# Cross-attention, first batch: other places for the first halves of ctx and of a weight, an earlier weight load, and fill transposes between the row dots

## The chip, the cores and the metric

The kernel runs on one core of one Trainium2 chip. The metric is the device time of one execution in microseconds, the median of several runs. Lower is better.

## The reference, cut to what matters

For x and ctx of shape (8, 512, 512) the first layer is a cross-attention with gate, all in fp32, and a second layer (an attention with experts) follows. Only the first batch of the first layer is touched.

```python
e = layernorm(x)                                             # the "encoder" rows, per batch
Sim = (e @ w1)[:, :, None] + (ctx @ w2)[:, None, :] + einsum('bid,bjd->bij', e * w3, ctx) + b_sim[0]
A = softmax(Sim, axis=2)
hq = einsum('bij,bjd->bid', A, ctx)
hc = einsum('bi,bid->bd', softmax(max(Sim, axis=2), axis=1), e)[:, None, :]
x1 = x + tanh(g_xattn[0]) * (concat([e, hq, e * hq, e * hc]) @ W_qv + b_qv)
out = x1 + tanh(g_ffn[0]) * ffn(layernorm(x1))               # second layer, not touched
```

## The kernel before, in words

Every product of 512 x 512 x 512 is made in three passes (PASSES): each fp32 operand is split into a high half, a rounded copy written by ScalarE (ACT), and a low half, the difference, written by VectorE (DVE) or GpSimd (POOL). So every operand costs one "hi" and one "lo" operation per tile, [128 x 512] each, before TensorE (PE) may read it. A product of one row tile is 12 matmuls of 128x512.

The order of each engine is written out by hand, and each engine runs it strictly in that order; semaphores tie them together. SP issues the DMAs in the order of its own program.

The first batch has its own order:

- SP loads x(0), ctx_t(0), small rows, ctx(0), the weight block wh_raw (it lives in `spare[:, 0]`), then the four tiles of x(1), each behind a wait for et_ps. Then it waits for ct_lo, for ew1_biased (the row dots with their bias, a DVE operation in `first_dots` of the vector engine), loads the residual (1 MB into x_sb), waits for c_lo = NT and loads weh_raw (1 MB) into `spare[:, 1]`, where ctx(0) lay before.
- PE turns the normalised rows (turn_e), makes the scores of four row tiles, turns the probabilities (turn_a), makes the row dots e @ w1 as matmuls with one column (`first_dots(t)`: four 128x1 matmuls for a tile; L932), and then `first_feats`: four products attend(k) into ps_h (k = 0 to 3, between them the small row_weights steps), then the products feats(t, part) with the weights wh, weh and wec. attend(k) for k >= 2 waits for eh_ready = k - 1, because ps_h has two banks.
- ACT writes the hi halves: ctx tiles 0 and 1 early, 2 and 3 late; then, behind the last probs_hi, the four tiles of wh, the four of e_t2 (rows_hi), the gate and the bias row, the four of weh; then `attended`: for each k a copy of ps_h (h_t2 hi), and the hi half of eh.
- DVE, in `attended`, writes the low half of h_t2 and the product eh, which is what releases ps_h (eh_ready).
- POOL writes the low halves of ctx, then, behind a wait for newton (the reciprocal root for batch 1, done by DVE), of wh, weh, and in turn of eh and e_t2.
- `fill(n)` issues n transposes of the identity into ps_b whose result nobody reads.

The wait that the load of the second weight stands behind, in SP's program:

```python
load_x(1, second=True)
sp.wait_ge(ct_lo, ND)
sp.wait_ge(ew1_biased, 1)
load_residual(0)
sp.wait_ge(c_lo, NT)
sp.dma_start(weh_raw[:], w_blocks[2]).then_inc(weh_loaded, 16)
```

Of the kernel before, what the change touches and what calls it, by code (L numbers as in the profile page):

```python
# [28 lines left out]
P = 128  # L29
# [81 lines left out]
def cross_attention(nc, block, both, x, ctx, ctx_t, g_xattn, w_sim, w_sim_cols, b_sim, w_qv, b_qv, x1, w_vsd, wq, wk):  # L111
# [7 lines left out]
    with ExitStack() as mem:  # L119
# [162 lines left out]
        def _(sp):  # L282
# [55 lines left out]
            load_first_ctx_t()  # L338
            sp.dma_start(w1_row[:], w_sim[0:D].partition_broadcast(P)).then_inc(dots_loaded, 16)
            sp.dma_start(bsim_col[:], b_sim.partition_broadcast(P)).then_inc(dots_loaded, 16)  # L340
            load_first_ctx()
            sp.dma_start(gate_raw[:], g_xattn.partition_broadcast(P)).then_inc(bias_loaded, 16)
            sp.dma_start(bias_row[:], b_qv.partition_broadcast(P)).then_inc(bias_loaded, 16)
            sp.dma_start(wh_raw[:], w_blocks[1]).then_inc(wh_loaded, 16)
            load_x(1, second=True)
            sp.wait_ge(ct_lo, ND)
            sp.wait_ge(ew1_biased, 1)
            load_residual(0)
            sp.wait_ge(c_lo, NT)
            sp.dma_start(weh_raw[:], w_blocks[2]).then_inc(weh_loaded, 16)  # L350

# [19 lines left out]
        def _(pool):  # L371
# [7 lines left out]
            def ctx_lo(b, first=False):  # L379
                for t in range(NT):  # L380
                    pool.wait_ge(c_hi, b * NT + t + 1)
                    take_lo(pool, c_2, t, weh_raw if first else stage).then_inc(c_lo, 1)
# [10 lines left out]
            def rows_lo(b):  # L393
                for k in range(ND):
                    row_lo(b, k)

# [18 lines left out]
            ctx_lo(0, True)  # L415
            pool.wait_ge(newton, 2 * ROOT_STEPS)
            weight_lo(wh, wh_raw, 0, range(ND))
            weight_lo(weh, weh_raw, ND, range(ND))
            for k in range(ND):
                scaled_lo(0, k)  # L420
                row_lo(0, k)
# [31 lines left out]
        def _(act):  # L453
# [31 lines left out]

            def softmax_exp(b, t):
                act.wait_ge(nmax_ready, b * NT + t + 1)
                if t >= 2:

                    act.wait_ge(at_ps, b * NT + t - 1)  # L490
                act.activation(a_sb[:, t % 2, :], ps_s[:, t % 2, :], ACT.Exp, bias=nmax[:, t:t + 1],
                               accum_out=den[:, t:t + 1]).then_inc(a_exp, 1)
# [16 lines left out]
            def attended(b, first, more):  # L509
# [4 lines left out]
                for k in range(ND):  # L514
# [8 lines left out]
                    act.activation(eh_t2[:, 0, k, :], tmp[:, k, :], ACT.Copy).then_inc(eh_hi, 1)  # L523
                for k in range(ND):
# [17 lines left out]
            def first_softmax():  # L542
# [4 lines left out]
                ctx_hi(0, True, (0, 1))  # L547
                first_scaled_hi(1)
                copy_e(0, 1, True)
                softmax_exp(0, 0)  # L550
# [7 lines left out]
                copy_e(0, 3, True)  # L558
                probs_hi(0, 1)
                softmax_exp(0, 2)  # L560
                normalise(0, 2)
                ctx_hi(0, True, (2, 3))
# [4 lines left out]
                weights_hi(wh, wh_raw, wh_loaded, range(ND))  # L567
                rows_hi(0, range(ND))
                act.wait_ge(bias_loaded, 2 * 16)
                act.activation(gate[:], gate_raw[:], ACT.Tanh).then_inc(gate_ready, 1)  # L570
                act.wait_ge(gate_ready, 1)
                act.activation(bias_row[:], bias_row[:], ACT.Copy, scale=gate[:, 0:1]).then_inc(bias_ready, 1)
# [31 lines left out]
        def _(dve):  # L604
# [50 lines left out]
            def first_scaled_lo(t):  # L655
                cols = slice(t * P, (t + 1) * P)
                dve.wait_ge(es_ready, t + 1)
                dve.wait_ge(es_hi, t + 1)
                dve.tensor_tensor(es_t2[:, 1, :, cols], tmp[:, :, cols], es_t2[:, 0, :, cols].bitcast(F32),  # L659
                                  ALU.subtract).then_inc(es_lo, 1)  # L660

# [59 lines left out]
            def first_softmax():  # L721
# [38 lines left out]
                for part in range(5, ROOT_PARTS):  # L760
                    root(1, part)

# [134 lines left out]
        def _(pe):  # L897
# [14 lines left out]
            def fill(times):  # L912

                for _ in range(times):
                    pe.transpose(ps_b[:, 0:P], ident[:], ident[:])
# [128 lines left out]
            def softmax(b, first):  # L1044
# [6 lines left out]
                for t in range(NT):  # L1051
# [6 lines left out]
                    if first and t == NT - 1:  # L1058
                        first_dots(1)
                        first_dots(2)  # L1060
                    turn_a(b, t, first)
                if first:
                    first_dots(NT - 1)
# [902 lines left out]
```

## Time and profile before

| | us |
|---|---|
| median of 3 runs | 1227.55 (1226.86 to 1227.98) |
| the profiled execution's own time | 1226.06 |
| its span, first to last instruction | 1224.3 |
| PE busy | 1192.7 (97%) |
| DVE, ACT, POOL busy | 832.2, 642.4, 661.9 |

The span is what the trace covers; 1.8 us of the profiled execution's time lie around it. All times in the trace are microseconds from the span's start. Durations in the profile's rows are those of one execution, which was 1.5 us below the median of the runs.

### The profile page before, as it was taken

The numbers are of one execution on the slowest core, as the hardware profiler recorded it, in microseconds if no ns is written. First come the engines' busy times: TensorE is split into PE (matmuls) and PEld (weight loads), VectorE is DVE, ScalarE is ACT, GpSimd is POOL, SyncE is SP. The second block draws the span as 40 slices with busy tenths as digits, with TensorE's granted clock in tenths as the row PEclk, the third lists the DMA queues.
The fourth block names the chain that finished last, engine by engine and source line by source line (L and its number), as shares of the span: only waits on it lengthen the run. The fifth ranks groups of instructions, "written<-read, shape, count | busy, mean of one in ns | idle before, by whom it ended". The sixth has DMA issues, their size and how long they took to land.

```text
span 1224.3 us, 19821 instructions
## 1 busy us (share of the span) xinstructions
PE 1192.7 (97%) x6406; PEld 920.1 (75%) x6406; DVE 832.2 (68%) x1530; ACT 642.4 (52%) x1431; POOL 661.9 (54%) x481
## 2 busy tenths in 40 slices
PE   7899999999999999999999999999999999999995
PEld 6688888888888888876877768777777777777663
DVE  7587777777777765566576574766765765865766
ACT  5443434343434343466666566566656666665661
POOL 1744242424242425239469388297496495693893
PEclk9799999999999999999999999999999999999998
DMA  5431313141313132420102003002002010010010
GB/s 190 138 121 52 121 52 126 46 129 43 129 43 129 43 95 78 150 76 1 35 1 83 20 0 103 0 17 86 0 35 68 0 69 34 0 69 0 0 69 35
DMA packets 40749, 75.92 MB, mean 62 GB/s; under 512 B 3728, under 2 KB 4240, under 8 KB 40720
## 3 DMA queue, kind: packets, MB, share of 16 engines
q1 hardware_dynamic: 40720, 75.55, 18.6%
q8 instruction: 16, 0.26, 0.1%
q14 instruction: 13, 0.11, 0.0%
HBM read 58.76 MB, written 16.78 MB: 62 GB/s over the span
## 4 chain that ended last, share of the span: by engine, by line
PE 91%; DVE 4%; issue 1%; ACT 1%; DMA 1%; POOLq 0%; POOL 0%; SPq 0%; DVEq 0%
PE ps_f L908 19%; PE ps_r L1802 15%; PE ps_s L1859 9%; PE ps_o L1872 9%; PE ps_s L1851 8%; PE ps_s L908 7%; PE ps_h L908 7%; PE ps_r L1811 6%; PE ps_r L1835 5%; PE ps_r L1817 1%; PE ps_t L961 1%; PE ps_r L1793 1%; PE ps_r L1825 1%; DMA spare<-in_w_qv 1%; PE ps_t L926 1%
## 5 line engine op out<-in xcount | busy, mean ns | idle before, releaser
L1564 DVE TENSOR_REDUCE nmax<-ps_s 128x1 f32<-128x512 f32 x256 | 158.7, 682 | 112.2 <-PE ps_s L1851 111.9
L1438 ACT ACTIVATE tmp<-ps_s,nmax 128x512 f32<-128x512 f32 x256 | 172.7, 688 | 106.7 <-DVE nmax L1564 106.7
L1399 POOL TENSOR_TENSOR z<-z,z_tmp 128x1280 f32<-128x1280 f32 x40 | 117.2, 2929 | 173.6 <-DVE z_tmp L1578 170.9
L1381 POOL TENSOR_TENSOR spare<-xv,pick 128x512 f32<-128x512 f32 x160 | 168.2, 1051 | 33.0 <-DVE pick L1673 19.9
L1387 POOL TENSOR_TENSOR spare<-spare 128x512 f32<-128x512 f32 x128 | 180.4, 1410 | 10.0
L1447 ACT ACTIVATE pt<-ps_s 128x512 f32<-128x512 f32 x256 | 132.4, 619 | 10.7 <-PE ps_s L1859 10.7
L1859 PE MATMUL ps_s<-ident,tmp 128*128 128x128 f32 x1024 | 125.0, 273 | 2.6 <-ACT tmp L1438 2.5
L1859 PEld LDWEIGHTS ps_s<-ident,tmp 128*128 128x128 f32 x1024 | 115.1, 140 | 13.6 <-ACT tmp L1438 6.9
L255 POOL TENSOR_TENSOR e_t<-e_t 128x512 fp32r<-128x512 f32 x32 | 40.7, 1298 | 141.5 <-ACT e_t L484 141.5
L1872 PE MATMUL ps_o<-pt,spare 128*64 128x512 f32 x512 | 116.9, 598 | 0.0
L1851 PE MATMUL ps_s<-k,q 64*128 64x512 f32 x768 | 106.9, 409 | 2.2 <-DVE k L1620 1.5
L908 PE MATMUL ps_h<-es_t,c 128*128 128x512 f32 x384 | 101.2, 415 | 4.3 <-DVE tmp L815 4.2
L1851 PEld LDWEIGHTS ps_s<-k,q 64*128 64x128 f32 x768 | 67.2, 184 | 46.2 <-issue 34.0
L1802 PE MATMUL ps_r<-es_t,wk 128*128 128x512 f32 x384 | 97.1, 401 | 0.0
L1802 PE MATMUL ps_r<-es_t,c_t 128*128 128x512 f32 x384 | 96.6, 400 | 0.0
L255 POOL TENSOR_TENSOR c<-stage,c 128x512 fp32r<-128x512 f32 x28 | 42.4, 1548 | 100.2 <-ACT c L251 100.2
L908 PE MATMUL ps_s<-c_t,es_t 128*128 128x512 f32 x384 | 93.8, 396 | 1.3 <-DVE es_t L659 1.2
L908 PE MATMUL ps_f<-weh,eh_t 128*128 128x512 f32 x384 | 94.7, 396 | 0.0
L908 PE MATMUL ps_f<-wh,h_t 128*128 128x512 f32 x384 | 93.7, 393 | 0.4 <-DVE x_sb L850 0.4
L908 PE MATMUL ps_f<-wec,e_t 128*128 128x512 f32 x384 | 92.3, 393 | 0.4 <-DVE wec L255 0.4
L908 PEld LDWEIGHTS ps_h<-es_t,c 128*128 128x128 f32 x384 | 73.2, 198 | 20.7 <-DVE tmp L815 4.3
L1802 PEld LDWEIGHTS ps_r<-es_t,wk 128*128 128x128 f32 x384 | 70.3, 188 | 21.0 <-issue 5.8
(198 smaller groups left out, 2114.3 us busy)
## 6 DMA issues: line engine op xcount, KB each, us to landing
stage<-in_x SPq DMA_DIRECT2D x32, 256.0 KB, 3.1
x_sb<-in_x SPq DMA_DIRECT2D x8, 1024.0 KB, 5.3
x_dram<-x_sb SPq DMA_DIRECT2D x32, 256.0 KB, 2.4
stage<-x_dram SPq DMA_DIRECT2D x8, 1024.0 KB, 5.6
x_sb<-x_dram SPq DMA_DIRECT2D x8, 1024.0 KB, 5.5
out_dram<-x_sb SPq DMA_DIRECT2D x32, 256.0 KB, 2.0
stage<-in_ctx_t SPq DMA_DIRECT2D x28, 256.0 KB, 3.0
stage<-in_ctx SPq DMA_DIRECT2D x28, 256.0 KB, 2.7
```

The source lines that it names most:

```text
L255: return eng.tensor_tensor(pair[:, 1, k, :], operand[:, k, :], pair[:, 0, k, :].bitcast(F32), ALU.subtract)
L908: last = pe.matmul(out, left(l, k), right(r, k), start=start and n == 1, stop=stop and n == ND * len(PASSES))
L1381: pool.tensor_tensor(v_tmp[:] if e else acc, xv[:, :, e, :].unsqueeze(2).broadcast_to(shape), pick[:, 0, e, :, 2 * p:2 * p + 2].unsqueeze( ...
L1387: pool.tensor_tensor(acc, acc, v_tmp[:], ALU.add).then_inc(v_steps, 1)
L1399: pool.tensor_tensor(zv, zv, z_tmp[:, h % 2], ALU.add).then_inc(z_pool, 1)
L1438: act.activation(probs[:, n % BANKS, :], ps_s[:, n % BANKS, :], ACT.Exp, bias=nmax[:, n:n + 1], accum_out=den[:, h, t:t + 1]).then_inc(p_e ...
L1447: act.activation(pt[:, h % 4, :, t * P:(t + 1) * P], ps_s[:, n % BANKS, :].rearrange("p (k t) -> p k t", k=NT), ACT.Copy).then_inc(pt_read ...
L1564: dve.tensor_reduce(nmax[:, n:n + 1], ps_s[:, n % BANKS, :], AX_X, ALU.max, negate=True).then_inc(nmax_ready, 1)
L1802: end = pe.matmul(ps, w2[:, l, k, n * P:(n + 1) * P], y_t2[:, r, k, :], start=m == 0, stop=m == len(every) - 1)
L1851: end = pe.matmul(ps_s[:, (n + a) % BANKS, :], q2[head_rows(a), p % 2, l, t * P:(t + 1) * P], k2[head_rows(a), p % 2, r, :], start=m == 0, ...
L1859: end = pe.transpose(ps_s[:, n % BANKS, k * P:(k + 1) * P], probs[:, n % BANKS, k * P:(k + 1) * P], ident[:])
L1872: end = pe.matmul(ps_o[head_rows(a), :], v_acc[:, p, k, a, :], pt[:, p % 2 * 2 + a, k, :], start=k == 0, stop=k == NT - 1)
```

## The change

It concerns the first batch of the cross-attention alone.

- SP: ctx(0) and wh_raw are issued ahead of the small rows (b_sim, w1, the gate, the bias); these come behind x(1). The load of weh_raw waits for c_lo = NT only, and the residual comes behind it; the wait for ew1_biased is gone.
- ACT: all four hi halves of ctx at once; the four of wh one by one at three earlier places; e_t2's hi halves are cut by row tiles (`first_row_hi(t)`, 128 columns of all four k) instead of by k, two of them behind the last probs_hi, two inside `attended`; gate and bias behind the k loop.
- POOL: a wait for es_lo = NT before ctx tiles 2 and 3; three low halves of wh ahead of the wait for newton; two row tiles of e_t2 (`first_row_lo`) instead of four tiles.
- DVE: the low halves of the other two row tiles of e_t2, read from PSUM, behind the reciprocal root of batch 1.
- PE: fifteen more fill transposes around the last row dots and turn_a(3); all fills write another quarter of ps_b.

```diff
--- before.py
+++ after.py
@@ -336,18 +336,17 @@
             load_x(0, True)
             sp.dma_start(w_cols[:], w_sim_cols).then_inc(cols_loaded, 16)
             load_first_ctx_t()
+            load_first_ctx()
+            sp.dma_start(wh_raw[:], w_blocks[1]).then_inc(wh_loaded, 16)
+            load_x(1, second=True)
+            sp.dma_start(bsim_col[:], b_sim.partition_broadcast(P)).then_inc(dots_loaded, 16)
             sp.dma_start(w1_row[:], w_sim[0:D].partition_broadcast(P)).then_inc(dots_loaded, 16)
-            sp.dma_start(bsim_col[:], b_sim.partition_broadcast(P)).then_inc(dots_loaded, 16)
-            load_first_ctx()
             sp.dma_start(gate_raw[:], g_xattn.partition_broadcast(P)).then_inc(bias_loaded, 16)
             sp.dma_start(bias_row[:], b_qv.partition_broadcast(P)).then_inc(bias_loaded, 16)
-            sp.dma_start(wh_raw[:], w_blocks[1]).then_inc(wh_loaded, 16)
-            load_x(1, second=True)
-            sp.wait_ge(ct_lo, ND)
-            sp.wait_ge(ew1_biased, 1)
-            load_residual(0)
             sp.wait_ge(c_lo, NT)
             sp.dma_start(weh_raw[:], w_blocks[2]).then_inc(weh_loaded, 16)
+            sp.wait_ge(ct_lo, ND)
+            load_residual(0)
             sp.wait_ge(w_lo, ND)
             sp.dma_start(we_raw[:], w_blocks[0]).then_inc(wraw_loaded, 16)
@@ -376,8 +375,8 @@
             pool.affine_select(out=ident[:], in_=ident[:], compare_op=ALU.not_equal, fill=1.0, base=0,
                                pattern=[[-1, P]], channel_multiplier=1).then_inc(ident_ready, 1)
-            def ctx_lo(b, first=False):
-                for t in range(NT):
+            def ctx_lo(b, first=False, tiles=range(NT)):
+                for t in tiles:
                     pool.wait_ge(c_hi, b * NT + t + 1)
                     take_lo(pool, c_2, t, weh_raw if first else stage).then_inc(c_lo, 1)
@@ -393,6 +392,12 @@
             def rows_lo(b):
                 for k in range(ND):
                     row_lo(b, k)
+
+            def first_row_lo(t, copies):
+                cols = slice(t * P, (t + 1) * P)
+                pool.wait_ge(et_hi, copies)
+                pool.tensor_tensor(e_t2[:, 1, :, cols], e_t[:, :, cols], e_t2[:, 0, :, cols].bitcast(F32),
+                                   ALU.subtract).then_inc(et_lo, 1)
             def scaled_lo(b, k):
                 pool.wait_ge(eh_hi, b * ND + k + 1)
@@ -412,13 +417,19 @@
             pool.wait_ge(es_lo, NT - 1)
-            ctx_lo(0, True)
+            ctx_lo(0, True, (0, 1))
+            pool.wait_ge(es_lo, NT)
+            ctx_lo(0, True, (2, 3))
+            weight_lo(wh, wh_raw, 0, (0, 1, 2))
             pool.wait_ge(newton, 2 * ROOT_STEPS)
-            weight_lo(wh, wh_raw, 0, range(ND))
+            weight_lo(wh, wh_raw, 0, (3,))
             weight_lo(weh, weh_raw, ND, range(ND))
-            for k in range(ND):
-                scaled_lo(0, k)
-                row_lo(0, k)
+            scaled_lo(0, 0)
+            scaled_lo(0, 1)
+            scaled_lo(0, 2)
+            first_row_lo(0, 3)
+            scaled_lo(0, 3)
+            first_row_lo(3, 4)
             pool.wait_ge(wec_ready, ND)
             add_bias(0, 0)
@@ -483,6 +494,10 @@
                 for k in tiles:
                     act.activation(e_t2[:, 0, k, :], e_t[:, k, :], ACT.Copy).then_inc(et_hi, 1)
+            def first_row_hi(t):
+                cols = slice(t * P, (t + 1) * P)
+                act.activation(e_t2[:, 0, :, cols], e_t[:, :, cols], ACT.Copy).then_inc(et_hi, 1)
+
             def softmax_exp(b, t):
                 act.wait_ge(nmax_ready, b * NT + t + 1)
                 if t >= 2:
@@ -521,6 +536,13 @@
                                        accum_out=bsum[:, 0:1]).then_inc(bexp_ready, 1)
                     act.wait_ge(eh_ready, b * ND + k + 1)
                     act.activation(eh_t2[:, 0, k, :], tmp[:, k, :], ACT.Copy).then_inc(eh_hi, 1)
+                    if first and k < 2:
+                        first_row_hi(3 * k)
+                if first:
+                    act.wait_ge(bias_loaded, 2 * 16)
+                    act.activation(gate[:], gate_raw[:], ACT.Tanh).then_inc(gate_ready, 1)
+                    act.wait_ge(gate_ready, 1)
+                    act.activation(bias_row[:], bias_row[:], ACT.Copy, scale=gate[:, 0:1]).then_inc(bias_ready, 1)
                 for k in range(ND):
                     act.wait_ge(wec_ready, b * ND + k + 1)
                     act.activation(wec[:, 0, k, :], tmp[:, k, :], ACT.Copy).then_inc(wec_hi, 1)
@@ -544,9 +566,10 @@
                     ctx_t_hi(0, k, True)
                 first_scaled_hi(0)
                 copy_e(0, 0, True)
-                ctx_hi(0, True, (0, 1))
+                ctx_hi(0, True)
                 first_scaled_hi(1)
                 copy_e(0, 1, True)
+                weights_hi(wh, wh_raw, wh_loaded, (0,))
                 softmax_exp(0, 0)
                 first_scaled_hi(2)
                 normalise(0, 0)
@@ -556,20 +579,17 @@
                 first_scaled_hi(3)
                 normalise(0, 1)
                 copy_e(0, 3, True)
+                weights_hi(wh, wh_raw, wh_loaded, (1,))
                 probs_hi(0, 1)
                 softmax_exp(0, 2)
                 normalise(0, 2)
-                ctx_hi(0, True, (2, 3))
+                weights_hi(wh, wh_raw, wh_loaded, (2, 3))
                 probs_hi(0, 2)
                 softmax_exp(0, 3)
                 normalise(0, 3)
                 probs_hi(0, 3)
-                weights_hi(wh, wh_raw, wh_loaded, range(ND))
-                rows_hi(0, range(ND))
-                act.wait_ge(bias_loaded, 2 * 16)
-                act.activation(gate[:], gate_raw[:], ACT.Tanh).then_inc(gate_ready, 1)
-                act.wait_ge(gate_ready, 1)
-                act.activation(bias_row[:], bias_row[:], ACT.Copy, scale=gate[:, 0:1]).then_inc(bias_ready, 1)
+                first_row_hi(1)
+                first_row_hi(2)
                 weights_hi(weh, weh_raw, weh_loaded, range(ND))
             first_softmax()
@@ -658,6 +678,12 @@
                 dve.wait_ge(es_hi, t + 1)
                 dve.tensor_tensor(es_t2[:, 1, :, cols], tmp[:, :, cols], es_t2[:, 0, :, cols].bitcast(F32),
                                   ALU.subtract).then_inc(es_lo, 1)
+
+            def first_row_lo(t, copies):
+                cols = slice(t * P, (t + 1) * P)
+                dve.wait_ge(et_hi, copies)
+                dve.tensor_tensor(e_t2[:, 1, :, cols], first_turned[t], e_t2[:, 0, :, cols].bitcast(F32),
+                                  ALU.subtract).then_inc(et_lo, 1)
             def row_dots(b):
                 for t in range(NT):
@@ -760,6 +786,9 @@
                 for part in range(5, ROOT_PARTS):
                     root(1, part)
+                first_row_lo(1, 1)
+                first_row_lo(2, 2)
+
             def softmax(b, more):
@@ -912,7 +941,7 @@
             def fill(times):
                 for _ in range(times):
-                    pe.transpose(ps_b[:, 0:P], ident[:], ident[:])
+                    pe.transpose(ps_b[:, P:2 * P], ident[:], ident[:])
             def turn_e(b, t, first=False):
                 pe.wait_ge(e_ready, b * NT + t + 1)
@@ -1056,10 +1085,14 @@
                     if first and t == 0:
                         first_dots(0)
                     if first and t == NT - 1:
+                        fill(3)
                         first_dots(1)
+                        fill(3)
                         first_dots(2)
+                        fill(3)
                     turn_a(b, t, first)
                 if first:
+                    fill(6)
                     first_dots(NT - 1)
                 else:
                     feats(b - 1, *LAST_FEATS[-1])
```

## Rows read from the trace of the kernel before

**Rows 1.** The page, part 1: busy time of each engine and its share of the span.
```profile
PE 1192.7 (97%) x6406; PEld 920.1 (75%) x6406; DVE 832.2 (68%) x1530; ACT 642.4 (52%) x1431; POOL 661.9 (54%) x481
```

**Rows 2.** The chain that ended last, in order of time: start us, us, what.
```profile
34.38 0.21 DVE ew L670
...
35.09 8.07 DMA spare<-in_w_qv
...
43.18 2.19 ACT weh L251 x4
```

**Rows 3.** The timeline of PE: start us, us, line, operation; idle before in brackets.
```profile
6.81 4.08 PE L915 MATMUL ps_b<-ident 128*128 128x128 f32 x18 [6.81 <-DVE stats L610]
...
12.51 1.47 PE L915 MATMUL ps_b<-ident 128*128 128x128 f32 x12
...
29.72 1.84 PE L932 MATMUL ps_b<-w_cols,e_t 128*128 128x1 f32 x16
...
32.19 0.66 PE L961 MATMUL ps_t<-ident,a_sb 128*128 128x128 f32 x4 [0.63 <-ACT a_sb L500]
...
32.68 1.64 PE L932 MATMUL ps_b<-w_cols,e_t 128*128 128x1 f32 x8
...
34.44 5.38 PE L908 MATMUL ps_h<-es_t,c 128*128 128x512 f32 x12
...
39.69 3.01 PE L908 MATMUL ps_h<-es_t,c 128*128 128x512 f32 x12
...
47.23 5.49 PE L908 MATMUL ps_h<-es_t,c 128*128 128x512 f32 x12 [4.22 <-DVE tmp L815]
...
56.62 3.00 PE L908 MATMUL ps_f<-wh,h_t 128*128 128x512 f32 x12
...
69.44 5.60 PE L908 MATMUL ps_f<-wec,e_t 128*128 128x512 f32 x24
```

**Rows 4.** Two windows of 0.5 us: PE, PEld, DVE, ACT, POOL busy, PEclk, DMA share, GB/s.
```profile
32.50:33.00 0.50, 0.50 (x7) 0.50 (x4) 0.43 (x5) 0.12 (x1) 0.00 (x0) 0.74 0.00 0
...
46.00:46.50 0.50, 0.00 (x0) 0.00 (x0) 0.50 (x2) 0.00 (x0) 0.50 (x2) 0.90 0.54 205
```

**Rows 5.** The chain, in the second batch: row_weights and the four attend products.
```profile
105.19 0.11 PE ps_b L978
...
117.98 2.77 PE ps_f L908 x12
```

**Rows 6.** The timeline of ACT.
```profile
14.54 1.14 ACT L251 ACTIVATE c<-spare 128x512 fp32r<-128x512 f32 x2
...
17.67 0.63 ACT L463 ACTIVATE es_t<-tmp 128x512 fp32r<-128x512 f32 x1 [1.98 <-DVE tmp L651]
...
19.73 0.69 ACT L491 ACTIVATE a_sb<-ps_s,nmax 128x512 f32<-128x512 f32 x1 [0.94 <-DVE nmax L693]
...
26.72 0.60 ACT L496 ACTIVATE es_t<-ps_t 128x512 fp32r<-128x512 f32 x1 [0.65 <-PE ps_t L961]
```

**Rows 7.** DMA issues of 0 to 90 us (all of ctx), at 9.92 and at 41.81: median us to landing.
```profile
spare<-in_ctx SPq DMA_DIRECT2D x4, 256.0 KB, 6.9
...
spare<-in_w_qv SPq DMA_DIRECT2D x1, 1024.0 KB, 8.7
...
spare<-in_w_qv SPq DMA_DIRECT2D x1, 1024.0 KB, 5.3
```

**Rows 8.** The timeline of POOL.
```profile
22.52 2.54 POOL L255 TENSOR_TENSOR c<-spare,c 128x512 fp32r<-128x512 f32 x2 [20.88 <-DVE es_t L659]
...
29.54 2.50 POOL L255 TENSOR_TENSOR c<-spare,c 128x512 fp32r<-128x512 f32 x2 [4.48 <-ACT c L251]
...
36.76 5.03 POOL L255 TENSOR_TENSOR wh<-spare,wh 128x512 fp32r<-128x512 f32 x4 [4.72 <-DVE rstd L71]
```

**Rows 9.** The timeline of DVE.
```profile
25.08 0.69 DVE L659 TENSOR_TENSOR es_t<-tmp,es_t 128x512 fp32r<-128x512 f32 x1
...
65.40 2.38 DVE L255 TENSOR_TENSOR wec<-tmp,wec 128x512 fp32r<-128x512 f32 x2
```

## The prediction

> **What bounds the kernel now.** The page comes first. PE is busy 97% of the span and no other engine over 68% [rows 1]: a saving counts only where PE itself waits or runs slowly, and what is saved there should last to the end, because from the second batch on PE never waits for long. So I look for PE's losses in the first 75 us.
>
> The chain of waits shows one loss plainly. The row dots get their bias in DVE at 34.38 to 34.59; behind that SP issues the residual and then the weight weh_raw, whose DMA lasts from 35.09 to 43.16; only then can ACT cast its four tiles, from 43.18 to 45.37 [rows 2]. ACT runs in order, so the copy of ps_h stands behind those casts, DVE's eh behind the copy, and PE's third attend product starts at 47.23, 4.22 us late [rows 3].
>
> The timeline of PE shows a second loss. attend(0) takes 5.38 us, attend(1) 3.01, attend(2) 5.49, with the same 12 matmuls [rows 3]. The granted clock fell within 32.5 to 33.0 (mean 0.74 of 2.4 GHz in that window) and again within 46.0 to 46.5 (0.90) [rows 4]. Before the first fall PE had issued 16 matmuls of one column and then waited 0.63 us [rows 3]; before the second it stood still.
>
> To size both together I take the stretch from attend(0) to the first feats product: 34.44 to 56.62 = 22.18 us [rows 3]. The same work in the second batch (four attends, four row_weights), at full clock and without a wait, takes 117.98 − 105.19 = 12.79 [rows 5]. The excess is 9.39 us: 4.22 of waiting and 5.2 of half clock.
>
> **The load (SP).** The new condition is c_lo = NT alone. ACT casts ctx tiles 2 and 3 right behind 0 and 1: 2 x 1.14 = 2.28 from 14.54, to 16.8 [rows 6]. The ctx tiles had landed about 6.9 after issues between 6 and 7.4, by 14.5, and the change issues them earlier [rows 7]. POOL writes tiles 0 and 1 from 22.52 to 25.06, waits for es_lo = NT (25.08 + 0.69 = 25.77) [rows 8, 9], and writes two more at 2.50: 28.3. A 1 MB weight load on an idle queue takes 5.3 [rows 7], so weh_raw lands at 33.7 instead of 43.16. The residual goes behind it and is read only by POOL's bias add, after 60 us. The small rows, moved behind x(1)'s last tile (released by a turn_e before 20 us), are on an idle queue and needed at 34.38 at the earliest.
>
> **ACT.** Each inserted operation has to fit a hole. ctx 2 and 3 end at 16.8; the next is at 17.67, which had 1.98 idle. wh tile 0 costs half of 1.14, at 18.7, with 0.94 idle before 19.73. wh tile 1 ends about when the copy at 26.72 began, with 0.65 idle. wh 2 and 3 take the very place that ctx 2 and 3 left [rows 6]. Cost zero; if a hole is gone, 0.6 each, at most 1.2 in all. After the last probs_hi (near 33.5) ACT has two row-tile casts at about 0.63, the price of the same strided shape [rows 6], and the four weh casts at 2.19 [rows 2]: done at 37.0, when attend(0) ends (37.2, below). So ACT is just in time. The two other row tiles and the gate, some 0.6 each, fall between the later k.
>
> **DVE.** The root ends where POOL's wait ended, 36.76 [rows 8]. Two new row-tile lows follow, a form that the trace lacks. Nearest is the strided low at 0.69 [rows 9]; I take that, 36.8 + 1.4 = 38.2, with gmax behind. Then h_lo and eh (0.69 each) give eh_ready(1) near 39.7. PE wants it for attend(2) at 37.2 + 0.3 + 2.8 = 40.3: 0.6 spare. At twice the price they cost PE 0.8; at nothing they gain nothing, for PE isn't waiting.
>
> **POOL.** ctx to 28.3, three wh tiles at 1.26 (5.03/4) to 32.1, idle to 36.8, one wh tile to 38.1, four weh tiles to 43.1 [rows 8]. That lets SP fetch the two remaining weights at 38.1 and 43.1, the last landing by 43.5 + 5.3 = 48.8 [rows 7]; DVE wants it near 52, after eh. The eh lows come in step with ACT (the fourth near 50.6), and the feats(0, 1) product that reads it starts about 6.4 after feats(0, 0), near 53.6. The e_t2 lows (unknown form, nearest 1.26, two of them) must be done by 60: even at three times the price they are hidden. So POOL has 3 us to spare at its tightest place.
>
> **PE's fills.** Twelve took 1.47, so 0.11 each, against 18 in 4.08, 0.23 each, before the clock had risen [rows 3]. Nine stand before turn_a(3): 1.0 us, of which the 0.63 idle covers most; turn_a(3) starts at about 32.4 to 32.5 instead of 32.19. Six more (0.66) and the last dots follow; these 8 took 1.64 at half clock, and 0.9 at the rate of the 16 in 1.84 [rows 3]: done at 34.5, against 34.44 for attend(0). Cost 0.1 at full clock. What they bring is that the clock doesn't fall. The trace can't show that directly. It shows that a stretch of dots and idle let it fall, and that the 12 fills of 12.51 followed by 1.2 us of idle didn't: the scores behind them ran at full rate. Nine fills amid 16 dots stand between the two; I take it that they hold it, because the dots' stretch then has more 128-column work than dots.
>
> For this there is a rule that speaks against. The trace: after 18 fills and 4 transposes of x alone, the fills went from 0.23 to 0.11 each [rows 3], so here transposes do wake the clock. The Trainium skill ("TensorE: Matmul & The Clock Gate", Part 4: PE-mode transpose) says that transpose mode isn't counted as PE being busy in the same way, so that the full clock doesn't engage. By the trace the sum is 9.3 us saved, by the rule 5.9 (the rival below); the trace disagrees with the rule as far as it goes.
>
> **The sum.** Excess of the stretch 9.39, less 0.1 for the later start: the first feats product comes 9.3 us earlier, near 47.3. From there to feats(0, 2) PE needs 12.82 (56.62 to 69.44); DVE's last wec was ready at 65.40 + 2.38 = 67.78, so 1.7 us ahead [rows 3, 9], and DVE's work moves with PE's. The saving stays whole. 1226.06 − 9.3 = 1216.8 for the profiled execution; that one was 1.5 under the median, so the median of the runs should come to **1218.2**. Its own range: from 1216.5 (a little more, or another draw of the median) to 1219.8 (0.8 for DVE, 0.6 for a lost hole).
>
> **Rivals.**
>
> *The clock falls all the same.* For it: nine fills are only 1 us within 3 us of dots and idle, and the skill's rule above. Against it: the transposes that woke the clock. Price: turn_a(3), six fills (0.23 each) and the dots (1.64) run at half clock, so attend(0) starts near 36.0; if the slow stretch again lasts to about 39.6, attend(0) is two thirds slow and ends near 40.6 where I have 37.2. That is 3.4 lost of 9.3: 5.9 saved, 1221.6. Chance 0.18.
>
> *DVE or ACT becomes what attend waits for.* With the attends at 2.9 us, DVE has 2 x 0.69, a normalise, and for k = 2 the batt steps, in each; ACT has two copies and a row tile. For it: spares of 0.6 to 0.8 us only. Against it: in the second batch the same DVE steps keep up. Price 1 to 3: 1219.2 to 1221.2. Chance 0.10.
>
> *The early load isn't early.* If c_lo still reaches NT at 32.04 as before (29.54 + 2.50) [rows 8], weh_raw lands at 37.4, casts end at 39.6, and the copy of ps_h is 2.4 late; if it stays in the order behind the residual, 2.7 more. Against it: nothing in the new order holds POOL. 1220.6 to 1224. Chance 0.04. That nothing at all changes (the wait just takes another name, the loss returns in the second batch) I give 0.03, 1227.5.
>
> *Slower: ACT's wait for wh_raw.* ACT now waits for wh_loaded ahead of the first exp at 19.73. Behind it stand all exps, probabilities and copies, and PE for all of them. The weight landed at 9.92 + 8.7 = 18.6 [rows 6, 7], and its place is good until 19.1; beyond that each us is lost one for one, and from 3 us of stall on PE stands and the clock falls too (2.5, as for attend(0)). It decides from about 26: stall 6.9 + 2.5 uses up the 9.3. At 29 it would be 9.9 + 2.5 − 9.3 = 3.1 slower, 1230.7. Against it: it is issued about 3 us sooner, with 0.5 MB fewer ahead of it. Chance 0.03.
>
> **How the numbers follow.** Forecast 0.62, the rivals 0.18, 0.10, 0.04, 0.03 and 0.03. Measurement can tell about 0.2%, 2.5 us, from no change: faster is all but the last two, less a part of the late load: 0.92; same 0.05; slower 0.03. The range goes from 1216.2 to 1222.2, which takes in the clock's case and most of DVE's; what is outside is about 0.15.
>
> **What the profile after would show.** The weh_raw issue near 28.4 and its casts over by 37.1; PEclk 1.00 through 30 to 55; attend(0) at 2.9 to 3.0 us; no idle before attend(2); the first feats product at 47.0 to 47.6. Wrong, if PEclk falls near 32.7 (then attend(0) near 5), if PE's wait moves to an eh or to an h_t low of DVE, if ACT shows idle before the casts of wh or weh with the DMA as releaser, or if the later batches show new waits of PE.

## The result, and the profile after

The changed kernel takes 1216.96 us (median of 5 runs, 1216.12 to 1218.32) against 1226.88 for the kernel before (5 runs): ratio 0.9919, 95% interval 0.9905 to 0.9934. The profiled execution is the one of 1216.96 us, its span 1215.1.

The page, part 1, of the changed kernel (answers to [rows 1]):

```profile
PE 1188.5 (98%) x6421; PEld 917.0 (75%) x6421; DVE 834.7 (69%) x1532; ACT 641.9 (53%) x1431; POOL 659.1 (54%) x479
```

PE's timeline of the changed kernel (answers to [rows 3]):

```profile
7.09 4.07 PE L944 MATMUL ps_b<-ident 128*128 128x128 f32 x18 [7.09 <-DVE stats L630]
...
32.69 0.60 PE L990 MATMUL ps_t<-ident,a_sb 128*128 128x128 f32 x4
...
34.74 3.02 PE L937 MATMUL ps_h<-es_t,c 128*128 128x512 f32 x12
...
37.62 3.01 PE L937 MATMUL ps_h<-es_t,c 128*128 128x512 f32 x12
...
40.87 3.06 PE L937 MATMUL ps_h<-es_t,c 128*128 128x512 f32 x12
...
47.54 3.00 PE L937 MATMUL ps_f<-wh,h_t 128*128 128x512 f32 x12
...
60.38 5.60 PE L937 MATMUL ps_f<-wec,e_t 128*128 128x512 f32 x24
...
66.43 3.06 PE L937 MATMUL ps_f<-wh,h_t 128*128 128x512 f32 x12 [0.45 <-DVE x_sb L879]
```

attend(0) takes 3.02 us where it took 5.38, attend(2) follows attend(1) with no idle, and the first feats product starts at 47.54 instead of 56.62: 9.08 us earlier. This execution began its statistics 0.28 later (first fill at 7.09, not 6.81: x(0) landed later), so the change's own part is 9.36. The spans differ by 9.2: what was won in the first 50 us is there at the end. The wait of 0.45 at 66.43 was there before (at 75.49) and is still there.

The same two windows as in [rows 4], PEclk the third figure from the right:

```profile
32.50:33.00 0.50, 0.50 (x6) 0.50 (x6) 0.47 (x3) 0.00 (x0) 0.00 (x0) 1.00 0.98 381
...
46.00:46.50 0.50, 0.50 (x3) 0.39 (x3) 0.50 (x2) 0.15 (x1) 0.35 (x1) 1.00 1.04 406
```

Neither fall is left. Now the load: SP's queue, the DMA from that issue to its landing, and ACT (answers to [rows 2, 6]).

```profile
28.74 0.38 SPq L347 DMA_DIRECT2D spare<-in_w_qv  x1
```

```profile
spare<-in_w_qv SPq DMA_DIRECT2D x1, 1024.0 KB, 5.2
```

```profile
19.01 0.62 ACT L251 ACTIVATE wh<-spare 128x512 fp32r<-128x512 f32 x1
...
26.30 0.62 ACT L251 ACTIVATE wh<-spare 128x512 fp32r<-128x512 f32 x1
...
34.86 2.18 ACT L251 ACTIVATE weh<-spare 128x512 fp32r<-128x512 f32 x4
...
37.80 0.60 ACT L531 ACTIVATE h_t<-ps_h 128x512 fp32r<-128x512 f32 x1 [0.75 <-PE ps_h L937]
```

The weight lands at 28.74 + 5.2 = 33.9 and ACT is done with its four casts at 37.04, 0.75 us before attend(0) lets go of ps_h. The casts of wh sit in holes of ACT, as said. POOL and DVE (answers to [rows 8, 9]):

```profile
26.17 2.54 POOL L255 TENSOR_TENSOR c<-spare,c 128x512 fp32r<-128x512 f32 x2 [0.80 <-DVE es_t L679]
...
28.67 3.76 POOL L255 TENSOR_TENSOR wh<-spare,wh 128x512 fp32r<-128x512 f32 x3
...
38.44 5.22 POOL L255 TENSOR_TENSOR weh<-spare,weh 128x512 fp32r<-128x512 f32 x4
...
50.83 1.31 POOL L399 TENSOR_TENSOR e_t<-e_t 128x512 fp32r<-128x512 f32 x1
```

```profile
37.02 1.28 DVE L685 TENSOR_TENSOR e_t<-ps_f,e_t 128x512 fp32r<-128x512 f32 x2
...
52.35 1.40 DVE L865 SCALAR_TENSOR_TENSOR tmp<-spare,hc 128x512 f32<-128x512 f32 x2
...
56.33 2.38 DVE L255 TENSOR_TENSOR wec<-tmp,wec 128x512 fp32r<-128x512 f32 x2
```

The two row-tile lows on DVE cost 1.28 together. The last wec low ends at 58.71, 1.67 ahead of feats(0, 2) at 60.38, the same spare as before.

### The profile page after: what moved, and what is told of

Same layout as the page of the kernel before. It is cut to its first block, busy times and chain, and to the rows that moved or that the text cites. A ratio compares the mean times of both kernels' runs of the same rounds, so it can differ in the third digit from the quotient of the medians.

```text
span 1215.1 us, 19851 instructions
## 1 busy us (share of the span) xinstructions
PE 1188.5 (98%) x6421; PEld 917.0 (75%) x6421; DVE 834.7 (69%) x1532; ACT 641.9 (53%) x1431; POOL 659.1 (54%) x479
## 4 chain that ended last, share of the span: by engine, by line
PE 93%; DVE 4%; issue 1%; ACT 1%; DMA 0%; POOLq 0%; POOL 0%; SPq 0%; DVEq 0%
PE ps_f L937 19%; PE ps_r L1835 15%; PE ps_s L1892 9%; PE ps_o L1905 9%; PE ps_s L1884 8%; PE ps_s L937 7%; PE ps_h L937 7%; PE ps_r L1844 6%; PE ps_r L1868 5%; PE ps_t L990 1%; PE ps_r L1850 1%; PE ps_r L1826 1%; PE ps_r L1858 1%; PE ps_t L955 1%; PE ps_b L1020 1%
## 5 line engine op out<-in xcount | busy, mean ns | idle before, releaser
L255 POOL TENSOR_TENSOR e_t<-e_t 128x512 fp32r<-128x512 f32 x28 | 35.3, 1291 | 138.5 <-ACT e_t L495 138.5
L1884 PEld LDWEIGHTS ps_s<-k,q 64*128 64x128 f32 x768 | 67.1, 184 | 46.3 <-issue 33.9
L937 PE MATMUL ps_h<-es_t,c 128*128 128x512 f32 x384 | 96.2, 400 | 0.0
L1835 PEld LDWEIGHTS ps_r<-es_t,c_t 128*128 128x128 f32 x384 | 69.7, 188 | 19.7 <-issue 5.8
```

Of the source, the lines that this page charges most:

```text
L255: return eng.tensor_tensor(pair[:, 1, k, :], operand[:, k, :], pair[:, 0, k, :].bitcast(F32), ALU.subtract)
L937: last = pe.matmul(out, left(l, k), right(r, k), start=start and n == 1, stop=stop and n == ND * len(PASSES))
L1835: end = pe.matmul(ps, w2[:, l, k, n * P:(n + 1) * P], y_t2[:, r, k, :], start=m == 0, stop=m == len(every) - 1)
L1884: end = pe.matmul(ps_s[:, (n + a) % BANKS, :], q2[head_rows(a), p % 2, l, t * P:(t + 1) * P], k2[head_rows(a), p % 2, r, :], start=m == 0, ...
```

## The experiments

The versions were timed in three groups, e1 to e4, then e5, e6, e7 and e11, then e8, e9, e10 and e12, each with runs of the kernel before beside it (median 1226.04, 1226.13 and 1225.44). So versions of different groups are compared by their ratios to the kernel before. The changed kernel's ratio is 0.9919 (0.9905 to 0.9934), against the five runs of the kernel before with the median 1226.88. That median is 0.8 to 1.4 us above those of the groups, as much as some of the losses below, so a loss against the changed kernel is also given inside a group: against e7_small_rows_first in the second, which differs from the changed kernel in the place of the small rows alone (1216.64), and against e10_fills_from_start in the third (1216.37).

Between profiled executions there is another difference: x(0) landed at different times, so that DVE's first operation of the root (L47) began at 7.39 in the kernel before, 7.69 in the changed kernel, and from 6.36 to 8.24 in the others. The head, the time from that operation to the start of feats(2, 0) on PE, leaves it out. It took 68.10 us in the kernel before (7.39 to 75.49) and 58.74 in the changed kernel (7.69 to 66.43).

| version | median us | ratio | 95% interval |
|---|---|---|---|
| e1_no_fills | 1218.44 | 0.9937 | 0.9923 to 0.9950 |
| e2_only_fills | 1226.32 | 0.9999 | 0.9990 to 1.0008 |
| e3_late_load | 1225.97 | 0.9998 | 0.9989 to 1.0007 |
| e4_only_load | 1222.35 | 0.9969 | 0.9958 to 0.9981 |
| e5_load_and_fills | 1222.39 | 0.9970 | 0.9959 to 0.9981 |
| e6_rows_by_k | 1219.00 | 0.9942 | 0.9928 to 0.9955 |
| e7_small_rows_first | 1216.64 | 0.9924 | 0.9910 to 0.9937 |
| e8_six_fills | 1220.03 | 0.9954 | 0.9941 to 0.9968 |
| e9_nine_fills | 1217.43 | 0.9935 | 0.9921 to 0.9948 |
| e10_fills_from_start | 1216.37 | 0.9924 | 0.9910 to 0.9938 |
| e11_wh_lows_late | 1219.87 | 0.9947 | 0.9933 to 0.9960 |
| e12_candidate | 1216.99 | 0.9931 | 0.9917 to 0.9944 |

### The fills alone taken away, and alone put in

e1_no_fills, from the changed kernel:

```diff
                     if first and t == NT - 1:
-                        fill(3)
                         first_dots(1)
-                        fill(3)
                         first_dots(2)
-                        fill(3)
                     turn_a(b, t, first)
                 if first:
-                    fill(6)
```

> The changed kernel without its fifteen new fills. Theory A (the fills hold the clock through the row dots): PEclk falls near 32 to 33 us, attend(0) takes about 5.3 us instead of 3.0, attend(1) ends near 43.0, and there is still no wait for the weight (its casts end at 37.0). About 2.4 us slower than the changed kernel: 1219.4, ratio to the kernel before 0.994. Rival B (fills, being transposes, count for nothing and the clock held for another reason): as the changed kernel, 1217.0, ratio 0.992, PEclk 1.00 throughout.

The timeline of PE and one window of its profiled execution:

```profile
34.01 5.49 PE L937 MATMUL ps_h<-es_t,c 128*128 128x512 f32 x12 [0.81 <-DVE es_t L734]
...
42.94 3.06 PE L937 MATMUL ps_h<-es_t,c 128*128 128x512 f32 x12
```

```profile
33.00:33.50 0.50, 0.20 (x2) 0.12 (x2) 0.47 (x3) 0.50 (x3) 0.00 (x0) 0.82 0.86 270
```

The clock fell within 33.0 to 33.5 (mean 0.82), attend(0) took 5.49 us, and there is no wait before attend(2). That is theory A in this execution; its head took 61.31 us (7.19 to 68.50), 2.57 more than the changed kernel's. By the ratios the loss is 0.0018 x 1226 = 2.2 us, but the two intervals overlap, so that number alone would not settle it. The mean granted clock of each of the five executions tells more: 0.993, 0.993, 0.996, 0.996 and 0.994, with times 1219.43, 1219.14, 1217.83, 1218.19 and 1218.44. The changed kernel had 0.996 or 0.997 in all five. A mean of 0.994 goes with a full fall (the profiled execution of e4_only_load has that mean, and its attend(0) took 4.85 us), so without the fills the clock fell in three executions and stayed in two: the fills don't only save some 2 us, they take a chance out.

e2_only_fills, from the kernel before: the same lines put in, and the other quarter of ps_b for fills.

> The kernel before with nothing but the fifteen fills (and the other quarter of ps_b for them). Theory A (two losses in series, one covers the other): attend(0) takes 3.0 us and attend(1) ends near 40.7, but the third attend still waits for the weight that lands near 43.3, so PE's wait grows from 4.2 to about 6.5 us and the time stays where it was, 1226.9 (ratio 0.999 to 1.001). Rival (the two losses add): 2.4 us faster, 1224.5, ratio 0.998.

```profile
34.37 3.04 PE L908 MATMUL ps_h<-es_t,c 128*128 128x512 f32 x12
...
47.23 5.10 PE L908 MATMUL ps_h<-es_t,c 128*128 128x512 f32 x12 [6.64 <-DVE tmp L815]
```

attend(0) took 3.04 us, and PE then waited 6.64 us instead of 4.22 for the same weight: the third product starts at 47.23, where it started before. The ratio is 0.9999. Fills alone are worth nothing, because the later wait covers what they save.

### The load alone taken back, and alone put in

e3_late_load, from the changed kernel:

```diff
-            sp.wait_ge(c_lo, NT)
-            sp.dma_start(weh_raw[:], w_blocks[2]).then_inc(weh_loaded, 16)
             sp.wait_ge(ct_lo, ND)
+            sp.wait_ge(ew1_biased, 1)
             load_residual(0)
+            sp.wait_ge(c_lo, NT)
+            sp.dma_start(weh_raw[:], w_blocks[2]).then_inc(weh_loaded, 16)
```

> The changed kernel with the load of the second weight where it was: behind the waits for ct_lo and ew1_biased and behind the residual. Theory A: the weight lands near 43.4, its casts end at 45.6, PE waits about 6.6 us before attend(2), the clock falls in that wait, and the whole gain is gone: 1226.5 to 1227, ratio 0.999 to 1.001. Rival (the earlier casts of ctx and wh on ACT and the row tiles carry a part of the gain themselves): 2 us or more stay, 1225 or less.

Measured 0.9998: nothing of the gain is left. PE waited 6.7 us before attend(2), which then took 5.49 us. The order on ACT, POOL and DVE, and the fills, are worth nothing without the early load.

e4_only_load: the kernel before with the reverse of that edit, and nothing else.

> The kernel before with only SP's order of the second weight changed: wait for c_lo alone, the residual behind it. c_lo reaches 4 at 32.04, so the weight lands at 37.4; ACT's old queue (wh, e_t2, gate, bias) ends at 38.5, the casts at 40.7, eh_ready(1) at 42.6, and attend(1) ends at 43.0 with the clock fallen in the dots as before. Theory A: no wait before attend(2), the second fall gone, 6.7 us faster, 1220.2, ratio 0.9945. Rival (ACT's and POOL's orders are needed for it): a wait of 1 us or more stays, with 4 us or less gained.

The expected 6.7 us are half missing: ratio 0.9969 is 3.8 us. In the profile attend(2) starts at 43.48 with no wait for eh, and the first feats product at 50.11, which is 6.5 earlier than before, though this execution began its root 0.85 later. So the theory held as far as it went, and the rest was given back behind it: the head took 63.91 us (8.24 to 72.15), 4.2 less than before. Its POOL, DVE and PE:

```profile
57.30 1.74 POOL L255 TENSOR_TENSOR e_t<-e_t 128x512 fp32r<-128x512 f32 x1
```

```profile
56.12 3.48 DVE L835 SCALAR_TENSOR_TENSOR tmp<-spare,hc 128x512 f32<-128x512 f32 x2
```

```profile
60.88 0.63 PE L925 MATMUL ps_t<-ident,stage 128*128 128x128 f32 x4 [1.41 <-ACT e_t L456]
...
62.15 0.63 PE L925 MATMUL ps_s<-ident,stage 128*128 128x128 f32 x4 [0.64 <-ACT e_t L456]
...
72.15 3.01 PE L907 MATMUL ps_f<-wh,h_t 128*128 128x512 f32 x12 [1.20 <-DVE x_sb L849]
```

POOL's queue (four lows of wh and four of weh behind the wait for newton, then eh and e_t2 in turn) runs until 59.0. DVE makes its first two wec products beside it: 3.48 us, where the changed kernel has 1.40. ACT casts wec behind DVE and copies the turned x(1) behind that, so PE waits 1.41, 0.64 and 1.20 us where the changed kernel waits 0.45 in all. DVE had no idle before or within the wec products, so it wasn't a late weight that held them. e4_only_load had 15.24 us from the first feats to feats(0, 2), the changed kernel 12.84.

e5_load_and_fills: both, on the kernel before.

> The kernel before with the early load of e4_only_load and the fifteen fills, ACT's and POOL's orders as before. In e4_only_load ACT's casts ended at 41.6 and eh_ready(1) came at 43.4, just when attend(1) ended; POOL's lows ended at 59.0 and DVE's first two wec products took 3.48 us together instead of 1.40 while POOL was busy. Theory A (what bounds e4_only_load is the queue of ACT, then POOL's): the fills make attend(0) 3.0 us, a wait of about 2 us before attend(2) takes their gain, and the time is that of e4_only_load, 1222.3 (ratio 0.997). Rival (fills and load add up to nearly the whole): 1219.5 or less, ratio 0.9945.

```profile
42.62 4.61 PE L907 MATMUL ps_h<-es_t,c 128*128 128x512 f32 x12 [1.92 <-DVE tmp L814]
```

The ratio is 0.9970, the same as with the load alone. The 1.92 us before attend(2) are ACT's old queue: its casts of weh end at 40.8, behind the four of wh, the four of e_t2, the gate and the bias, and the copy of ps_h stands behind them. The fall of the clock that the fills prevent in the dots comes back inside that very product (4.61 us). That wait and that fall, 3.5 us together, are what ACT's new order can save here; no run puts that order alone in or takes it alone out.

### POOL's queue and the row tiles

e11_wh_lows_late, from the changed kernel:

```diff
-            weight_lo(wh, wh_raw, 0, (0, 1, 2))
             pool.wait_ge(newton, 2 * ROOT_STEPS)
-            weight_lo(wh, wh_raw, 0, (3,))
+            weight_lo(wh, wh_raw, 0, range(ND))
```

> The changed kernel with all four wh lows of POOL behind its wait for newton, as before. POOL then ends 3.8 us later, near 55.9, and the last two weights are fetched later (the last lands near 52.8 instead of 48.9). Theory A (e4_only_load gave back its gain through POOL's late queue: a late weight and DVE's products slowed by a busy POOL): 1.5 to 2.5 us slower than the changed kernel, ratio 0.9935 to 0.994, feats(0, 0) still near 47.5 but a wait of PE later, between it and feats(0, 2). Rival (the spare of 1.7 us hides it): within 0.5 us of the changed kernel, ratio 0.992.

```profile
52.67 3.41 DVE L864 SCALAR_TENSOR_TENSOR tmp<-spare,hc 128x512 f32<-128x512 f32 x2
```

```profile
57.38 0.63 PE L954 MATMUL ps_t<-ident,stage 128*128 128x128 f32 x4 [0.84 <-ACT e_t L467]
```

Ratio 0.9947: 3.4 us lost against the changed kernel, 3.2 against e7_small_rows_first beside it (the profile accounts for 2.6: from feats(0, 0) to feats(0, 2) 14.67 us instead of 12.84, and 1.20 instead of 0.45 at the wait behind). feats(0, 0) started at 47.17, on time. The first two wec products took 3.41 us, with no idle of DVE before or within them. Of the two causes in theory A it is the busy POOL, not a late weight.

e6_rows_by_k, from the changed kernel: `rows_hi(0, range(ND))` on ACT in place of the four first_row_hi, `row_lo(0, k)` in turn with `scaled_lo(0, k)` on POOL, and DVE's two first_row_lo gone.

> The changed kernel with e_t2 split as before: four casts on ACT behind the last probs_hi, four lows on POOL, none on DVE. ACT's weh casts end 1.1 us later (38.1), eh_ready(1) near 40.6 against attend(1)'s end at 40.9, POOL ends 2.6 us later, near 54.7. Theory A (the spares hold): no change within 0.5 us, ratio 0.992 to 0.9925. Rival (POOL's longer queue runs into DVE's wec products, as in e4_only_load): 1 to 2 us of the gain are lost, ratio 0.993 to 0.994, with a wait of PE before the turns of x(1).

```profile
51.89 1.47 POOL L255 TENSOR_TENSOR e_t<-e_t 128x512 fp32r<-128x512 f32 x1
```

```profile
50.56 1.65 DVE L635 TENSOR_SCALAR stage<-stage,mean,rstd 128x512 f32<-128x512 f32 x1
...
52.13 2.44 DVE L856 SCALAR_TENSOR_TENSOR tmp<-spare,hc 128x512 f32<-128x512 f32 x2
```

```profile
57.25 0.63 PE L946 MATMUL ps_s<-ident,stage 128*128 128x128 f32 x4 [0.74 <-ACT e_t L465]
...
67.25 3.06 PE L928 MATMUL ps_f<-wh,h_t 128*128 128x512 f32 x12 [1.17 <-DVE x_sb L870]
```

Here my theory missed and the rival held. Ratio 0.9942, some 2.8 us lost, 2.4 against e7_small_rows_first (the profile accounts for 1.7). ACT was in time, as expected. But POOL ran until 53.4, and beside it DVE's normalise took 1.65 us and the two wec products 2.44, against 1.24 and 1.40. Two lows moved to DVE cost DVE 1.28 us at a place where nothing waits, and take a busy POOL from beside operations that PE does wait for.

### The small rows, and which fills

e7_small_rows_first, from the changed kernel: b_sim, w1, gate and bias issued ahead of ctx and wh_raw again.

> The changed kernel with the small rows of SP ahead of ctx and wh as before, so wh_raw lands near 18.6 instead of 15. Its first cast stands at 19.0. Theory A: nothing waits, 1217, ratio 0.992. Rival: the landing comes after 19.1 in some executions and holds ACT and then the scores, up to 1 us.

Ratio 0.9924, no difference that can be measured. In its profile ACT waited 0.49 us for wh_raw before its first cast at 18.23, and the exp behind it began at 18.77. The exp had no idle left before it, where the changed kernel's had 0.43. The landing uses up the hole, so the early issue buys safety and no time that can be measured.

e8_six_fills keeps only `fill(6)`, e9_nine_fills only the three `fill(3)`.

> The changed kernel with the six fills behind turn_a(3) alone; the nine amid the dots are gone. Theory A (the nine hold the clock through the long stretch of dots): the clock falls near 33 as in e1_no_fills, and the six fills, now at half rate, delay attend(0) a little more: 1218.5 to 1219.5, ratio 0.9935 to 0.9945. Rival (what counts is the last stretch before attend(0)): as the changed kernel, ratio 0.992.

> The changed kernel with the nine fills amid the dots and without the six behind turn_a(3). Theory A: the clock holds, and nothing is lost, since attend(0) waits for DVE's at_lo anyway: ratio 0.992, attend(0) at 3.0 us. Rival: the 8 dots and the wait before attend(0) are enough to let it fall: ratio 0.994.

```profile
31.87 1.49 PE L944 MATMUL ps_b<-ident 128*128 128x128 f32 x6
```

e8_six_fills: 0.9954, the clock fell in all five executions (means 0.993 to 0.994) and the six fills ran at half rate, as the row shows, ahead of attend(0); it is no better than e1_no_fills. e9_nine_fills: 0.9935; four executions had a mean of 0.996, one 0.993, and that one was the slowest by 0.9 us. The head of its profiled execution, one of the four, took as long as the changed kernel's, 58.74 us. Its interval takes in the changed kernel's ratio, so whether the six are worth anything beyond the chance isn't settled.

By the means, the clock fell in 14 of 17 executions of the early-load versions with no fills amid the dots (e1_no_fills, e4_only_load, e8_six_fills) and in 1 of 5 with nine. The mean clock of every execution of the fifteen-fill versions whose load is early (the changed kernel, e6_rows_by_k, e7_small_rows_first, e10_fills_from_start, e11_wh_lows_late, e12_candidate) was 0.996 or 0.997, 30 of 30. What no run separates is whether it counts that the fills are work of 128 columns or only that they leave PE less idle.

### Two attempts at more

e10_fills_from_start, from the changed kernel:

```diff
+            fill(30)
             pe.wait_ge(stats_done, 3)
             fill(18)
+            pe.wait_ge(newton, ROOT_STEPS - 3)
+            fill(3)
```

> The changed kernel with thirty fills as soon as the identity is there (1.7 us) and three behind the first root, so that PE is at full clock when the first turn_e comes. Theory (transposes wake the clock wherever they stand): turn_e(0, 0) takes 0.6 us instead of 1.1 and the whole kernel moves forward by 0.5 to 0.7 us: 1216.4, ratio 0.9915. Rival (fills at this place wake nothing, or they end too late and hold turn_e up): as the changed kernel, 0.992, or slower.

PE, then DVE:

```profile
1.69 6.94 PE L944 MATMUL ps_b<-ident 128*128 128x128 f32 x48 [1.69 <-POOL ident L375]
...
10.78 0.66 PE L955 MATMUL ps_t<-ident,stage 128*128 128x128 f32 x4 [0.63 <-DVE stage L641]
```

```profile
11.69 1.37 DVE L671 TENSOR_SCALAR tmp<-ps_t,w_cols 128x128 f32<-128x128 f32 x4
```

The first turn_e of the changed kernel, and of e11_wh_lows_late, which like it has only the 18 fills ahead of it:

```profile
11.29 1.11 PE L955 MATMUL ps_t<-ident,stage 128*128 128x128 f32 x4
```

```profile
11.15 0.66 PE L954 MATMUL ps_t<-ident,stage 128*128 128x128 f32 x4 [0.24 <-DVE stage L640]
```

The 48 fills took 6.94 us, 0.14 each, where 18 alone take up to 0.23 each and those behind a risen clock 0.12: the rate rose among transposes, with nothing else on PE. (PEclk reads 1.00 throughout these first microseconds in every trace, so here the rate is read from durations.) But the first turn_e at 0.66 us instead of 1.11 isn't the new fills' doing: e1_no_fills, e2_only_fills, e7_small_rows_first and e11_wh_lows_late, with the 18 fills alone, have 0.66 too. Nor is what follows from it. DVE's first scaled rows start at 11.69, right behind a c_t low that stands ahead of them in DVE's order; from the first operation of the root to the first scores it took 7.60 us where the changed kernel's profiled execution took 7.84, and e11_wh_lows_late 7.59. Ratio 0.9924, the same as e7_small_rows_first: no gain.

e12_candidate, from e10_fills_from_start:

```diff
-            pool.wait_ge(wec_ready, ND)
+            pool.wait_ge(ew1_ready, 2 * NT)
             add_bias(0, 0)
```

> e10_fills_from_start with POOL's three bias adds moved behind DVE's row dots of batch 1 (they wait for those instead of for the wec products). Theory (a busy POOL slows some of DVE's operations: the first two row dots take 1.8 us each beside POOL and 0.7 without): all four row dots at 0.7, DVE 2 us ahead at the residual, and PE's wait of 0.45 before feats(2, 0) goes: 0.4 to 0.5 us better than e10_fills_from_start, ratio 0.991. Rival (the slowing moves to the scaled rows that follow, three of 0.54 us): no better or slower than e10_fills_from_start.

```profile
59.51 1.36 DVE L700 TENSOR_SCALAR ew<-ew,bsim_col 128x4 f32<-128x4 f32 x1
...
60.79 3.03 DVE L659 TENSOR_SCALAR tmp<-e_t,w_cols 128x512 f32<-128x512 f32 x2
```

The row dots took 0.69 each, but the bias of the dots took 1.36 and the two scaled rows 3.03 beside POOL (0.23 and 1.00 in e10_fills_from_start); PE waited 0.53 before feats(2, 0). The rival held: the slowing only moved. Neither version is measurably better than the changed kernel.

## Why the prediction was right

**The excess of 9.39 us** as the measure of what there is to win held: 9.36 by the profile, 9.9 by the medians.

**The weight's landing** was put at 33.7, measured 33.9. Its steps came as worked out: c_lo at 28.7 (said 28.3), the load 5.2 (said 5.3). The row of the 1 MB load on an idle queue was the right one to take. e3_late_load shows that this edit is necessary for all of the gain. One reading beside it was off without harm: POOL's bias adds, which read the residual, began at 56.49 and not after 60; the residual had landed at 37.2.

**ACT just in time**: casts done at 37.04 (said 37.0). **DVE's row tiles**: 1.28 for two (said 1.4), eh_ready(1) at 39.72 (said 39.7). **POOL's fourth eh low**: ended at 50.9 (said near 50.6).

**The fills** hold the clock, which was the disputed step (chance 0.62 against 0.18). e1_no_fills, e8_six_fills and e9_nine_fills show it. The reason given for it, that the trace of before showed transposes waking the clock, held too: in e10_fills_from_start they did so alone. The rule of the Trainium skill ("TensorE: Matmul & The Clock Gate", Part 4: PE-mode transpose) that transposes don't count in the same way is not borne out for these fp32 transposes by the identity: nine amid the dots kept the clock in 4 of 5 executions and fifteen in 30 of 30, where it held in 3 of 17 with none there. The price of 3.4 for fills whose clock falls all the same was near: e8_six_fills, where six fills run at half rate ahead of attend(0), lost 4.3 by the ratios, 3.7 against e10_fills_from_start beside it and 2.9 by the heads (61.63); e1_no_fills, with no fills to run slowly, lost 2.2 by the ratios. The fall that one rival put at "from 3 us of stall on" rests on one wait of 4.22 us; in e5_load_and_fills the clock fell at 43.0 to 43.5, behind a wait of 1.92.

**What was right by its number and too light in its reasons**: I gave POOL's new order a price of zero and called the e_t2 lows hidden "even at three times the price". The place where they end was as said, but I asked only who waits for POOL's results. e11_wh_lows_late and e6_rows_by_k show that POOL's being busy is itself a cost: 3.4 and 2.8 us by the ratios, 2.6 and 1.7 by the profiles, which the intervals of the ratios still hold. These edits were part of the change, so the number came out although their worth was left out of the sum: the sum took for granted that DVE keeps its pace behind feats(0, 0), and that was luck as far as its reasons go. So the change's parts are not a load, fills and some tidying. The load opens the gain; ACT's earlier casts let attend(2) start at once (shown by the 1.92 us of e5_load_and_fills, not by a run of its own); POOL's early lows and DVE's row tiles keep the gain from being given back 15 us later; the fills add some 2 at the end, and only when the others are there (e5_load_and_fills: nothing).

The median forecast was 1218.2 and came to 1216.96. Of this 1.2, some 0.7 are the median of the kernel before, which came out 0.7 lower over five runs than over three; the rest is within what runs of one kernel differ by.

## What to carry to other kernels

Losses in series on one chain hide one another: fills alone gave 0.0 us and the load alone 3.8, while together with an order that feeds them they gave 9.4 by the profile. Take the stretch's own cost in an undisturbed batch as the measure, and follow each engine's queue to the next meeting point before pricing one edit. An engine with slack is not free to load: before moving work to POOL, look at what DVE does at that time, and put DVE's operations on PSUM there. A few transposes between matmuls of one column are cheap insurance for the clock, and the mean granted clock of every execution, not one profile, shows whether it is needed.

## What the runs showed of the hardware

**DVE beside a busy POOL.** With both engines at work, some of DVE's operations of 128x512 are stretched, others not. Stretched: the normalise (TENSOR_SCALAR, SBUF to SBUF) from about 0.54 to as much as 1.65; the wec products (two inputs in SBUF) from 1.40 to 3.48 for two; the row dots (two in SBUF) from 0.69 to 1.78. Not stretched: the same kind of dot with one input in PSUM, 0.68 beside POOL, and the h_t lows and eh products with an input in PSUM, 0.68. In each full case the addition is 1.0 to 1.1 us per operation, whatever the operation's own length (the bias of the dots in e12_candidate, 0.23 to 1.36; a scaled row, 0.50 to 1.51): less than one POOL operation beside it (1.3 to 1.7). So an estimate counts DVE's operations under POOL's chain, not their busy time. That POOL is the cause and not a bystander is shown by e12_candidate: with its adds moved, the row dots went back to 0.69 and the operations now beside it were stretched. The Trainium skill ("SBUF — State Buffer", Who interferes with whom) says the same: an operation of DVE with two SBUF inputs contends with a GpSimd instruction that reads SBUF, one in a mode that uses both of DVE's port pairs contends with GpSimd, and one with at most one SBUF input outside those modes doesn't. The trace of before had shown it already (its last normalise, beside POOL, took 1.23 us), and the prediction didn't use it.

**The clock's fall is a matter of chance where PE has little to do.** The clock of the same kernel without fills fell in some executions and not in others, and in the profiled ones it came within 32.5 to 33.0 in the kernel before, within 33.0 to 33.5 in e1_no_fills and near 32.5 in e4_only_load. Its first rise varies as well: of the twelve profiled executions with 18 fills ahead of the first turn_e, four took 0.66 us for it and six 1.08 to 1.12. So the cost of a fall, or the worth of an early rise, must be read from several executions.
